# Queries and keys of a pair as one tile of 1024 columns in two neighbouring banks, and the cosine product placed behind the scaling of the scores on VectorE

## The chip, the cores and the metric

The kernel runs on one core of a Trainium2 chip. The metric is the device time of one execution in microseconds (us), and the time of a kernel is the median of its runs.

## What is computed

The reference is a macaron block on x of 8 sequences, 256 positions and 128 features, all in float32: half a transformer, a selective scan, and half a transformer with the same weights.

```python
x = x + 0.5 * _L0_ffn_ref(_layernorm(x, axis=-1), ...)
x = x + _L0_attn_ref(_layernorm(x, axis=-1), ...)
x = x + 0.5 * _L0_ffn_ref(_layernorm(x, axis=-1), ...)
```

`_L0_ffn_ref` is six layers, each an attention and a gated feed-forward layer. The attention is what the change touches:

```python
qkv = x @ Wqkv
q, k, v = jnp.split(qkv, 3, -1)
q = l2norm(q) * qs
k = l2norm(k) * ksc
q = q * cos * scale + rotate_half(q) * sin * scale
k = k * cos * inv + rotate_half(k) * sin * inv
out = local_attention(q, k, v)      # windows of 32, each sees itself and the one before
return out.transpose(0, 2, 1, 3).reshape(b, n, INNER) @ Wo
```

It has 16 heads of 64 features. `_L0_attn_ref` is layer norm, two projections, a short convolution, a scan over 16 states and an output projection.

## The kernel before

Features lie on the 128 partitions and tokens on the columns. The 2048 tokens are cut into 4 chunks of two sequences (512 columns). An **item** is one chunk in one layer, so that a stack (one of the two half transformers, k = 0 and 1) has 24 items. A **pair** is two heads, and an item has 8 pairs.

The whole stack is one pipeline of **steps**, 8 to an item, written out in advance: `Step(t)` says which piece of which item every engine does at step t, and each engine's program walks the same list (`tensor_stack`, `vector_stack`, `scalar_stack`, `gpsimd_stack`) in an order written by hand. The engines meet only through semaphores, and each takes its instructions strictly in this order. Step t projects pair p = t % 8 of item n = t // 8 (`st.now`). At every even step the attention of a **group** of four heads, projected 10 steps before, enters the pipeline:

- TensorE computes the scores (`pe_scores`, L719) onto banks that ScalarE has filled with the mask (`act_mask`, L1137).
- VectorE multiplies them by the inverse norms of the keys (`dve_scores`, L940) and takes the row maximum (`dve_max`, L946).
- Then follow GpSimd (subtract, scale), ScalarE (exponential, L1162), VectorE (`dve_sums`, L952), GpSimd again and the transpose `dve_turn` (L966), over the next steps.
- At the even step 4 steps later TensorE multiplies the probabilities by the values (`pe_values`, L692), and ScalarE copies the result (`act_att`, L1155).

What the text calls steps 0 to 7 is p. All even steps carry the scores of one group and the values of an earlier one. In addition, step 0 has the statistics of the norms of q and k on VectorE (`dve_norms`), step 1 `act_norms`, `dve_norms_back` (L922 to L927), half of the output projection (`pe_out`, L668) and the gates of the feed-forward layer; steps 2 and 3 the value half of it (`dve_hidden`, L973), step 4 its output (`pe_ffn_out`, added by L980 on VectorE), step 5 the other half of `pe_out`, steps 6 and 7 the layer norm.

For one pair and one step: TensorE projects the queries at the top of the step and the keys late in it (`pe_project`, three matmuls of 512 columns each, L656 to L658), each into one bank. ScalarE squares each (`act_square`, L1085). VectorE then makes two products out of each (`dve_rotate`): with the sine table into `sines` (L868), and with the cosine table into the ring of rotated queries or keys (L874). Four DMAs of SyncE move the sine products to their partner partitions, and GpSimd adds them (`pool_rotate`, L1259). Late in each step TensorE projects the values (`pe_v`, L749 to L751), and VectorE transposes them (`dve_v`, L891).

PSUM has 8 banks of 512 columns. One holds the sums of squares. The other seven are given out in a fixed rotation by the class `Banks`, in the order in which TensorE uses them: `use(key, sem, value)` gives the next bank and remembers which semaphore says that it has been read, and TensorE waits for the reader of the bank's last holder before it writes (`pe_bank`). `pe_values` takes four banks (one for each j) and waits for all four before its first matmul:

```python
            if blocks[0] == 0:
                for j in range(4):
                    pe_bank(w, ("att", k, n, group, j))
```

## Time and profile before

| | |
|---|---|
| median of 3 runs | 3368.71 us (3358.27 to 3374.22) |
| span of the profiled execution | 3373.6 us |
| TensorE busy | 2905.4 us (86%) |
| VectorE busy | 2981.4 us (88%) |
| GpSimd busy | 2425.2 us (72%) |
| ScalarE busy | 2061.4 us (61%) |

The profiled execution's own time is its span; it stands 4.9 us above the median of the runs. The busy shares are means over the whole span, with the scan between the two stacks in it (some 330 us), where other code runs. A matmul's record begins when it is taken up and its end is modelled, so that a busy TensorE is not TensorE at its peak.

### The profile page before, as it was taken

To read this page: it belongs to the slowest core of one execution; us is meant where nothing else is said; L and a number is where in the kernel's file an instruction comes from. 1 tells how busy PE (TensorE), PEld (TensorE's weight loads), DVE (VectorE), ACT (ScalarE), POOL (GpSimd) and SP (SyncE) were. 2 spreads that over 40 slices of the span, in tenths; PEclk is the share of its full clock that TensorE was granted. 3 is DMA by queue.
4 is the path that set the end of the run, shared out by engine and by line. 5 is a ranking of instruction groups with operands and counts; after the bars stand their busy time and mean duration, and the time that the engine had idled before them with its cause. 6 is when DMAs were issued, how large, how long until landed. Compare 5 with 4: busy or idle time off the path is not lost. (4 is left out here: it accounts for less than half of the span.)

```text
span 3373.6 us, 132100 instructions
## 1 busy us (share of the span) xinstructions
PE 2905.4 (86%) x57914; PEld 1846.3 (55%) x57914; DVE 2981.4 (88%) x4200; ACT 2061.4 (61%) x3820; POOL 2425.2 (72%) x1679
## 2 busy tenths in 40 slices
PE   5788889989989899987767788998999988999987
PEld 3455555655655555653323455565566655565653
DVE  6789899999999899896898878989999989899994
ACT  3466566666666665664764456666666666566663
POOL 3678777787787687774454667778788787787773
PEclk8899999999999999998887889999999999999998
DMA  5233332333333333320001333333343333333330
GB/s 140 65 83 73 82 91 68 89 90 72 86 92 71 84 85 71 83 72 28 7 7 44 80 72 79 75 87 86 75 97 76 90 84 72 81 94 71 86 76 14
DMA packets 114726, 250.85 MB, mean 74 GB/s; under 512 B 27244, under 2 KB 60648, under 8 KB 114152
## 3 DMA queue, kind: packets, MB, share of 16 engines
q1 hardware_dynamic: 114152, 242.40, 30.3%
q8 instruction: 457, 7.49, 1.0%
q14 instruction: 117, 0.96, 0.1%
HBM read 37.82 MB, written 3.15 MB: 12 GB/s over the span
## 5 line engine op out<-in xcount | busy, mean ns | idle before, releaser
L1085 ACT ACTIVATE squares<-general 128x512 f32<-128x512 f32 x768 | 453.9, 597 | 720.8 <-PE general L658 712.2
L1279 POOL TENSOR_TENSOR probs<-probs,row_sum 128x1024 f32<-128x1024 f32 x192 | 365.3, 1903 | 426.3 <-DVE row_sum L957 425.5
L1259 POOL TENSOR_TENSOR q_ring<-q_ring,partner 128x512 f32<-128x512 f32 x384 | 491.1, 1279 | 216.6 <-DMA partner<-sines 216.3
L868 DVE SCALAR_TENSOR_TENSOR sines<-general,vec,consts 128x512 f32<-128x512 f32 x768 | 560.7, 730 | 68.4 <-ACT squares L1085 65.5
L1259 POOL TENSOR_TENSOR k_ring<-k_ring,partner 128x512 f32<-128x512 f32 x384 | 490.8, 1278 | 0.0
L692 PE MATMUL general<-probs_t,v_buf 32*64 32x64 f32 x24576 | 339.4, 236 | 158.3 <-issue 87.0
L656 PE MATMUL general<-xs_hi,wqkv_lo 128*128 128x512 f32 x768 | 457.3, 595 | 15.8 <-DVE xs_lo L897 7.6
L692 PEld LDWEIGHTS general<-probs_t,v_buf 32*64 32x64 f32 x24576 | 305.6, 135 | 248.8 <-issue 241.7
L1273 POOL TENSOR_TENSOR probs<-probs,q_scale 128x1024 f32<-128x1024 f32 x192 | 365.3, 1903 | 15.1
L668 PE MATMUL general<-att,wo 128*128 128x512 f32 x768 | 370.4, 627 | 6.5 <-ACT att L1155 5.2
L719 PE MATMUL general<-k_ring,q_ring 64*32 64x64 f32 (+1 forms) x24576 | 294.2, 224 | 88.4 <-issue 53.5
L1265 POOL TENSOR_TENSOR probs<-probs,row_max 128x1024 f32<-128x1024 f32 x192 | 366.5, 1909 | 0.1
L719 PEld LDWEIGHTS general<-k_ring,q_ring 64*32 64x32 f32 x24576 | 260.0, 106 | 122.6 <-issue 103.4
L657 PE MATMUL general<-xs_lo,wqkv_hi 128*128 128x512 f32 x768 | 315.7, 411 | 2.7 <-issue 2.7
L658 PE MATMUL general<-xs_hi,wqkv_hi 128*128 128x512 f32 x768 | 314.5, 409 | 0.7 <-issue 0.5
L656 PEld LDWEIGHTS general<-xs_hi,wqkv_lo 128*128 128x128 f32 x768 | 153.7, 200 | 264.6 <-issue 233.4
L1155 ACT ACTIVATE att<-general 128x256 f32<-128x256 f32 x768 | 231.3, 388 | 97.0 <-PE general L692 95.6
L891 DVE STREAM_TRANSPOSE v_buf<-general 128x512 f32<-128x512 f32 x384 | 265.3, 691 | 27.1 <-PE general L751 27.0
L874 DVE SCALAR_TENSOR_TENSOR k_ring<-general,vec,consts 128x512 f32<-128x512 f32 x384 | 285.1, 742 | 0.0
L874 DVE SCALAR_TENSOR_TENSOR q_ring<-general,vec,consts 128x512 f32<-128x512 f32 x384 | 284.6, 741 | 0.0
L730 PE MATMUL sums<-squares,consts 128*32 128x512 f32 x1536 | 248.4, 612 | 40.4 <-ACT squares L1085 36.1
L952 DVE TENSOR_REDUCE row_sum<-probs 128x16 f32<-128x1024 f32 x192 | 230.6, 1201 | 41.2 <-ACT probs L1162 41.0
(232 smaller groups left out, 6348.2 us busy)
## 6 DMA issues: line engine op xcount, KB each, us to landing
partner<-sines SPq DMA_DIRECT2D x1536, 128.0 KB, 2.3
wqkv_raw<-in_wqkv SPq DMA_DIRECT2D x80, 208.0 KB, 2.7
wo<-in_wo SPq DMA_DIRECT2D x12, 512.0 KB, 5.1
w<-in_w SPq DMA_DIRECT2D x12, 341.0 KB, 3.2
base_dram<-x SPq DMA_DIRECT2D x8, 256.0 KB, 2.4
att<-in_wqkv SPq DMA_DIRECT2D x2, 1024.0 KB, 6.1
sines<-base_dram SPq DMA_DIRECT2D x8, 256.0 KB, 4.0
w<-in_w SPq DMA_DIRECT2D x12, 128.0 KB
```

What stands on the lines that cost most here:

```text
L656: e.matmul(g[:, :], wqkv_lo[:, p, cut], xs_hi[:, r, :], start=True, stop=False)
L657: e.matmul(g[:, :], wqkv_hi[:, p, cut], xs_lo[:, r, :], start=False, stop=False)
L668: done = e.matmul(g[:, :], wo[:, p, :], att[:, p, :], start=(p == OUT_PAIRS[i][0]), stop=(p == OUT_PAIRS[i][-1]))
L692: done = e.matmul(o, lhs, rhs, start=(kb == 0), stop=True, skip_group_check=True)
L719: done = e.matmul(o, qw, kw, start=False, stop=True, skip_group_check=True)
L868: e.scalar_tensor_tensor(out=by_seq(sines[:, i % 2, which, :]), in0=g, scalar=scale, in1=both(tables[:, 2 * which + 1, :]), op0=ALU.mult, ...
L874: e.scalar_tensor_tensor(out=by_seq(qk_ring[which][:, slot_of(n, p), :]), in0=g, scalar=scale, in1=both(tables[:, 2 * which, :]), op0=ALU. ...
L1085: e.activation(squares[:, (2 * p + which) % 4, :], general_of(("proj", k, n, p, which))[:, :], ACT.Square).then_inc(S[f"squared_{side}"], 1)
L1259: e.tensor_tensor(y, y, partner[:, i % 2, which, :], ALU.add).then_inc(S[f"rotated_{side}"], 1)
L1265: e.tensor_tensor(y, y, spread_keys(row_max[:, i % 2, :]), ALU.subtract).then_inc(S["max_off"], 1)
L1273: e.tensor_tensor(y, y, spread_keys(q_scale8[:, n % 2, group, :]), ALU.mult).then_inc(S["q_norms_off"], 1)
L1279: e.tensor_tensor(y, y, spread_keys(row_sum[:, i % 2, :]), ALU.mult).then_inc(S["probs_done"], 1)
```

## The change

The queries and keys of a pair become one tile of 1024 columns. `Banks.use` takes a width: a tile of two banks needs two neighbours (and skips the last bank of the rotation where only that one is left), and its first matmul waits for the readers of both. TensorE projects queries and keys directly behind each other at the top of the step, with one signal behind both. ScalarE squares both in one instruction, and GpSimd adds the partners of both in one. On VectorE the scale vector moves into a copy of the tables, made once a layer (`dve_tables`, two instructions), so that each product is a plain multiplication, and one instruction makes the sine products of both (`dve_sin`), another the cosine products (`dve_cos`). `dve_cos` stands behind `dve_scores`, which in turn is one instruction of 1024 columns instead of two of 512; the mask copy likewise. The two banks of the projection are released by the semaphore `cos`. To make room, `inv_norm` and two weights of the scan share memory with other tiles, and the loads of the scan's weights stand at the end of SyncE's list of the first stack.

```diff
-    def use(self, key, sem, value):
-        at = self.next
-        self.next = (at + 1) % self.banks
-        self.of[key], self.before[key], self.filled[key] = at, self.last.get(at), self.written.get(at, False)
-        self.last[at] = (sem, value)
-        self.written[at] = key[0] in ("proj", "v", "spread", "scores", "project", "ffn_out", "center", "var")\
-            or key[0] in ("gate", "value") and HIDDEN_CUTS[key[3]][1] == P
+    def use(self, key, sem, value, width=1):
+
+        at = self.next if self.next + width <= self.banks else 0
+        self.next = (at + width) % self.banks
+        taken = range(at, at + width)
+        self.of[key], self.before[key] = at, [self.last[i] for i in taken if i in self.last]
+        self.filled[key] = all(self.written.get(i, False) for i in taken)
+        for i in taken:
+            self.last[i] = (sem, value)
+            self.written[i] = key[0] in ("proj", "v", "spread", "scores", "project", "ffn_out", "center", "var")\
+                or key[0] in ("gate", "value") and HIDDEN_CUTS[key[3]][1] == P
...
-                self.use(("proj", k, n, p, 0), "cos_q", (g + n) * PAIRS + p + 1)
+                self.use(("proj", k, n, p), "cos", (g + n) * PAIRS + p + 1, 2)
...
-                for seq in range(CHUNK_SEQS):
-                    self.use(("scores", k, n, group, seq), "k_norms_off", ((g + n) * GROUPS + group) * 2 + seq + 1)
+                self.use(("scores", k, n, group), "k_norms_off", (g + n) * GROUPS + group + 1, CHUNK_SEQS)
...
-            if st.now:
-                n, p = st.now
-                self.use(("proj", k, n, p, 1), "cos_k", (g + n) * PAIRS + p + 1)
...
-        qk_ring = [sb("q_ring", [P, RING, COLS]), sb("k_ring", [P, RING, COLS])]
+        qk_ring = sb("qk_ring", [P, RING, 2, COLS])
+        layer_tables = sb("layer_tables", [P, 2, 2, SEQ])
...
+        inv_norm = k_inv[:, WIN:]
...
+        ring = banks("general", POOL_BANKS)
+        general = [ring[:, i * COLS:(i + 1) * COLS] for i in range(POOL_BANKS)]
+        sums = banks("sums", 1)
...
-        mw = sb("mw", [P, 4, P])
-        wbc = sb("wbc", [P, P])
+        raw_words = wqkv_raw.rearrange("p i c -> p (i c)")
+        mw = raw_words[:, 0:4 * P].rearrange("p (m n) -> p m n", m=4)
+        wbc = raw_words[:, 4 * P:5 * P]
...
+        def two_of(key):
+            at = BANKS.index(key)
+            return ring[:, at * COLS:(at + 2) * COLS]
...
+            if k == 0:
+                w.wait_ge(S["wqkv_lo"], DEPTH * PAIRS)
+                e.dma_start(mw, mw_in.rearrange("m d n -> d m n")).then_inc(S["m_loaded"], 16)
+                e.dma_start(wbc, wb_in).then_inc(S["m_loaded"], 16)
+                e.dma_start(mvec[:, :], mvec_in).then_inc(S["m_loaded"], 16)
...
-            w.wait_ge(S["sin_q"], i + 1)
-            w.wait_ge(S["sin_k"], i + 1)
-
-            w.wait_ge(S["rotated_q"], i - 1)
-            w.wait_ge(S["rotated_k"], i - 1)
+            w.wait_ge(S["sin"], i + 1)
+
+            w.wait_ge(S["rotated"], i - 1)
...
         def pe_bank(w, key):
-            before = BANKS.free(key)
-            if before:
-                w.wait_ge(S[before[0]], before[1])
+            for sem, value in BANKS.free(key):
+                w.wait_ge(S[sem], value)
             return general_of(key)
...
-        def pe_project(e, w, k, n, p, which):
+        def pe_project(e, w, k, n, p):
+
             m, r = k * ITEMS + n, n % 2
-            g, cut = pe_bank(w, ("proj", k, n, p, which)), slice(which * P, (which + 1) * P)
+            pe_bank(w, ("proj", k, n, p))
             w.wait_ge(S["xs_lo"], m + 1)
             w.wait_ge(S["wqkv_lo"], (k * DEPTH + n // CHUNKS) * PAIRS + p + 1)
-            e.matmul(g[:, :], wqkv_lo[:, p, cut], xs_hi[:, r, :], start=True, stop=False)
-            e.matmul(g[:, :], wqkv_hi[:, p, cut], xs_lo[:, r, :], start=False, stop=False)
-            e.matmul(g[:, :], wqkv_hi[:, p, cut], xs_hi[:, r, :], start=False, stop=True)\
-                .then_inc(S[f"proj_{SIDE[which]}"], 1)
+            for which in range(2):
+                g, cut = two_of(("proj", k, n, p))[:, which * COLS:(which + 1) * COLS], slice(which * P, (which + 1) * P)
+                e.matmul(g, wqkv_lo[:, p, cut], xs_hi[:, r, :], start=True, stop=False)
+                e.matmul(g, wqkv_hi[:, p, cut], xs_lo[:, r, :], start=False, stop=False)
+                done = e.matmul(g, wqkv_hi[:, p, cut], xs_hi[:, r, :], start=False, stop=True)
+            done.then_inc(S["proj"], 1)
...
                 if st.now:
-                    pe_project(e, w, k, *st.now, 0)
+                    pe_project(e, w, k, *st.now)
...
-                if st.now:
-                    pe_project(e, w, k, *st.now, 1)
                 if st.values:
...
-        def dve_rotate(e, w, k, n, p, which):
-            m, side, layer = k * ITEMS + n, SIDE[which], n // CHUNKS
-            i = m * PAIRS + p
-            g, scale = by_seq(general_of(("proj", k, n, p, which))[:, :]), vcol(layer, V_QS + which)
+        def by_side(a):
+            return a.rearrange("p w (s t) -> p w s t", s=CHUNK_SEQS)
+
+        def layer_table(part):
+            return layer_tables[:, :, part, :].unsqueeze(2).broadcast_to([P, 2, CHUNK_SEQS, SEQ])
+
+        def dve_tables(e, w, k, layer):
+
             w.wait_ge(S["vec_loaded"], 16)
-            w.wait_ge(S[f"squared_{side}"], i + 1)
+            w.wait_ge(S["cos"], (k * ITEMS + layer * CHUNKS) * PAIRS)
+            for which in range(2):
+                e.tensor_scalar(layer_tables[:, which, :, :], tables[:, which, :, :], vcol(layer, V_QS + which), None, ALU.mult)\
+                    .then_inc(S["tables_scaled"], 1)
+
+        def dve_sin(e, w, k, n, p):
+            i = (k * ITEMS + n) * PAIRS + p
+            if p == 0 and n % CHUNKS == 0:
+                dve_tables(e, w, k, n // CHUNKS)
+            w.wait_ge(S["tables_scaled"], 2 * (k * DEPTH + n // CHUNKS + 1))
+            w.wait_ge(S["squared"], i + 1)
 
             w.wait_ge(S[f"moved{i % 2}"], i // 2 * 64)
-            e.scalar_tensor_tensor(out=by_seq(sines[:, i % 2, which, :]), in0=g, scalar=scale, in1=both(tables[:, 2 * which + 1, :]),
-                                   op0=ALU.mult, op1=ALU.mult).then_inc(S[f"sin_{side}"], 1)
+            g = by_side(two_of(("proj", k, n, p)).rearrange("p (w c) -> p w c", w=2))
+            e.tensor_tensor(by_side(sines[:, i % 2, :, :]), g, layer_table(1), ALU.mult).then_inc(S["sin"], 1)
+
+        def dve_cos(e, w, k, n, p):
+            g = by_side(two_of(("proj", k, n, p)).rearrange("p (w c) -> p w c", w=2))
 
             held = n * PAIRS + p - RING
             if held >= 0:
                 w.wait_ge(S["scored"], (k * ITEMS + held // PAIRS) * GROUPS + held % PAIRS // 2 + 1)
-            e.scalar_tensor_tensor(out=by_seq(qk_ring[which][:, slot_of(n, p), :]), in0=g, scalar=scale,
-                                   in1=both(tables[:, 2 * which, :]), op0=ALU.mult, op1=ALU.mult).then_inc(S[f"cos_{side}"], 1)
+            e.tensor_tensor(by_side(qk_ring[:, slot_of(n, p), :, :]), g, layer_table(0), ALU.mult).then_inc(S["cos"], 1)
...
-            for seq in range(CHUNK_SEQS):
-                start = k_inv[:, seq * SEQ:seq * SEQ + 1]
-                keys = bass.AP(start.tensor, start.offset, [list(start.ap[0]), [WIN, NWIN], [1, 2 * WIN]])
-                y = probs[:, i % PROBS, seq * COLS:(seq + 1) * COLS]
-                e.tensor_tensor(cube(y), cube(general_of(("scores", k, n, group, seq))[:, :]), keys, ALU.mult).then_inc(S["k_norms_off"], 1)
+            start = k_inv[:, 0:1]
+            keys = bass.AP(start.tensor, start.offset, [list(start.ap[0]), [WIN, ITEM_WINS], [1, 2 * WIN]])
+            e.tensor_tensor(cube(probs[:, i % PROBS, :]), cube(two_of(("scores", k, n, group))), keys, ALU.mult).then_inc(S["k_norms_off"], 1)
...
                 if st.now:
-                    dve_rotate(e, w, k, *st.now, 0)
+                    dve_sin(e, w, k, *st.now)
                 if st.scale:
                     dve_scores(e, w, k, *st.scale)
+                if st.now:
+                    dve_cos(e, w, k, *st.now)
...
-                if st.now:
-                    dve_rotate(e, w, k, *st.now, 1)
...
-        def act_square(e, w, k, n, p, which):
-            i, side = (k * ITEMS + n) * PAIRS + p, SIDE[which]
-            w.wait_ge(S[f"proj_{side}"], i + 1)
+        def act_square(e, w, k, n, p):
+            i, at = (k * ITEMS + n) * PAIRS + p, 2 * (p % 2)
+            w.wait_ge(S["proj"], i + 1)
             w.wait_ge(S["squares_summed"], i // 2)
-            e.activation(squares[:, (2 * p + which) % 4, :], general_of(("proj", k, n, p, which))[:, :], ACT.Square).then_inc(S[f"squared_{side}"], 1)
+            e.activation(squares[:, at:at + 2, :].rearrange("p w c -> p (w c)"), two_of(("proj", k, n, p)), ACT.Square).then_inc(S["squared"], 1)
...
-        def pool_rotate(e, w, k, n, p, which):
-            i, side = (k * ITEMS + n) * PAIRS + p, SIDE[which]
-            y = qk_ring[which][:, slot_of(n, p), :]
+        def pool_rotate(e, w, k, n, p):
+            i = (k * ITEMS + n) * PAIRS + p
+            y = qk_ring[:, slot_of(n, p), :, :]
             w.wait_ge(S[f"moved{i % 2}"], (i // 2 + 1) * 64)
-            w.wait_ge(S[f"cos_{side}"], i + 1)
-            e.tensor_tensor(y, y, partner[:, i % 2, which, :], ALU.add).then_inc(S[f"rotated_{side}"], 1)
```

TensorE at step 2 of an item in the middle of a stack. L764 is the first matmul of the feed-forward layer's value half, L656 to L658 are the projection of the keys, L692 is `pe_values`, L749 the projection of v. Before:

```order
L764 MATMUL general<-centered,w 128x512 [waits gelu_done]
L656 MATMUL general<-xs_hi,wqkv_lo 128x512 [waits cos_k]
L657 MATMUL general<-xs_lo,wqkv_hi 128x512
L658 MATMUL general<-xs_hi,wqkv_hi 128x512
L692 MATMUL general<-probs_t,v_buf 64x64 [waits k_inv_kept,cos_q,k_norms_off,v_kept,probs_turned]
L692 MATMUL general<-probs_t,v_buf 64x64 x55
L692 MATMUL general<-probs_t,v_buf 64x32 x8
L749 MATMUL general<-xs_hi,wqkv_lo 128x256 [waits k_norms_off]
```

After the change (L741 is the spread of the norms, L722 the scores, L767 the value half, L696 `pe_values`, L752 the projection of v):

```order
L741 MATMUL general<-inv_parts,spread_sel 128x256
L722 MATMUL general<-qk_ring 32x32 [waits mask_set,rotated]
L722 MATMUL general<-qk_ring 32x32 x7
L722 MATMUL general<-qk_ring 32x64 x56
L767 MATMUL general<-centered,w 128x512 [waits gelu_done]
L696 MATMUL general<-probs_t,v_buf 64x64 [waits cos,k_inv_kept,v_kept,probs_turned]
L696 MATMUL general<-probs_t,v_buf 64x64 x55
L696 MATMUL general<-probs_t,v_buf 64x32 x8
L752 MATMUL general<-xs_hi,wqkv_lo 128x256 [waits k_norms_off]
```

The projection of the keys is gone from the place between the value half and `pe_values`; it stands at the top of the step. Among the semaphores for which `pe_values` waits, `cos` of this same step stands where `cos_q` and `k_norms_off` of this step stood.

VectorE at step 4, from the top of the step. L868 and L874 are the sine and cosine products, L940 is `dve_scores`, L980 adds the feed-forward output, L952 is `dve_sums`, L891 `dve_v`. Before:

```order
L868 SCALAR_TENSOR_TENSOR sines<-general,vec,consts 128x512 [waits moved0,squared_q]
L874 SCALAR_TENSOR_TENSOR q_ring<-general,vec,consts 128x512
L940 TENSOR_TENSOR probs<-general,k_inv 128x512 [waits k_inv_kept,probs_turned,scored]
L940 TENSOR_TENSOR probs<-general,k_inv 128x512
L980 SCALAR_TENSOR_TENSOR x<-general,vec,x 128x512 [waits shifted,ffn_done]
L868 SCALAR_TENSOR_TENSOR sines<-general,vec,consts 128x512 [waits squared_k]
L874 SCALAR_TENSOR_TENSOR k_ring<-general,vec,consts 128x512
L952 TENSOR_REDUCE row_sum<-probs 128x16 [waits exponent]
L891 STREAM_TRANSPOSE v_buf<-general 128x16x32 [waits v_projected]
L957 RECIPROCAL row_sum<-row_sum 128x16 [waits row_sum]
```

After the change (L884 and L892 are the sine and cosine products, L955 `dve_scores`, L995 the addition, L967 `dve_sums`, L908 `dve_v`):

```order
L884 TENSOR_TENSOR sines<-general,layer_tables 128x1024 [waits moved0,squared]
L955 TENSOR_TENSOR probs<-general,k_inv 128x1024 [waits k_inv_kept,probs_turned,scored]
L892 TENSOR_TENSOR qk_ring<-general,layer_tables 128x1024
L995 SCALAR_TENSOR_TENSOR x<-general,vec,x 128x512 [waits shifted,ffn_done]
L967 TENSOR_REDUCE row_sum<-probs 128x16 [waits exponent]
L908 STREAM_TRANSPOSE v_buf<-general 128x16x32 [waits v_projected]
L972 RECIPROCAL row_sum<-row_sum 128x16 [waits row_sum]
L961 TENSOR_REDUCE row_max<-probs 128x16 [waits max_off,k_norms_off]
```

Four products of 512 columns became two of 1024; the cosine product moved from ahead of the scaling of the scores to behind it.

## Rows read from the trace of the kernel before

**Rows 1.** Windows of core 0: busy us of each engine, granted clock, DMA share, GB/s

```profile
20.00:170.00 150.00, 103.23 (x1642) 68.27 (x1642) 115.72 (x174) 67.91 (x137) 81.81 (x59) 0.84 0.36 85
300.00:1400.00 1100.00, 990.41 (x21260) 645.92 (x21259) 1010.48 (x1440) 706.97 (x1333) 849.11 (x583) 0.96 0.35 81
```

**Rows 2.** Groups of VectorE by form, 300 to 1400 us: count | busy, mean ns | idle before

```profile
L868 DVE SCALAR_TENSOR_TENSOR sines<-general,vec,consts 128x512 f32<-128x512 f32 x284 | 207.4, 730 | 14.1 <-ACT squares L1085 13.0
```

**Rows 3.** Timeline of VectorE, 899 to 960 us: start, duration, instruction, [idle before it <-releaser]

```profile
899.77 1.28 DVE L940 TENSOR_TENSOR probs<-general,k_inv 128x512 f32<-128x512 f32 x2
...
903.87 1.22 DVE L952 TENSOR_REDUCE row_sum<-probs 128x16 f32<-128x1024 f32 x1 [0.84 <-ACT probs L1162]
...
913.82 1.28 DVE L940 TENSOR_TENSOR probs<-general,k_inv 128x512 f32<-128x512 f32 x2
915.01 0.74 DVE L980 SCALAR_TENSOR_TENSOR x<-general,vec,x 128x512 f32<-128x512 f32 x1
915.67 0.74 DVE L868 SCALAR_TENSOR_TENSOR sines<-general,vec,consts 128x512 f32<-128x512 f32 x1
916.33 0.75 DVE L874 SCALAR_TENSOR_TENSOR k_ring<-general,vec,consts 128x512 f32<-128x512 f32 x1
916.99 1.21 DVE L952 TENSOR_REDUCE row_sum<-probs 128x16 f32<-128x1024 f32 x1
918.11 0.71 DVE L891 STREAM_TRANSPOSE v_buf<-general 128x512 f32<-128x512 f32 x1
...
918.87 1.17 DVE L946 TENSOR_REDUCE row_max<-probs 128x16 f32<-128x1024 f32 x1
919.95 0.74 DVE L868 SCALAR_TENSOR_TENSOR sines<-general,vec,consts 128x512 f32<-128x512 f32 x1
...
927.12 1.28 DVE L940 TENSOR_TENSOR probs<-general,k_inv 128x512 f32<-128x512 f32 x2
...
932.63 0.72 DVE L891 STREAM_TRANSPOSE v_buf<-general 128x512 f32<-128x512 f32 x1 [0.90 <-PE general L751]
...
941.23 1.28 DVE L940 TENSOR_TENSOR probs<-general,k_inv 128x512 f32<-128x512 f32 x2
...
950.59 1.00 DVE L922 CAST norm_t<-norm_t 128x128 fp32r<-128x128 f32 x1
...
959.10 1.28 DVE L940 TENSOR_TENSOR probs<-general,k_inv 128x512 f32<-128x512 f32 x2
```

**Rows 4.** Timeline of TensorE, 935 to 949 us: start, duration, instruction

```profile
935.50 1.08 PE L730 MATMUL sums<-squares,consts 128*32 128x512 f32 x8
936.51 0.50 PE L656 MATMUL general<-xs_hi,wqkv_lo 128*128 128x512 f32 x1
...
937.64 1.48 PE L719 MATMUL general<-k_ring,q_ring 64*32 64x32 f32 x128
...
941.57 1.57 PE L692 MATMUL general<-probs_t,v_buf 32*64 32x64 f32 x128 [1.56 <-DVE q_ring L874]
943.07 0.39 PE L749 MATMUL general<-xs_hi,wqkv_lo 128*128 128x256 f32 x1
...
943.88 0.40 PE L656 MATMUL general<-xs_hi,wqkv_lo 128*128 128x512 f32 x1
...
944.58 3.65 PE L668 MATMUL general<-att,wo 128*128 128x512 f32 x8
```

**Rows 5.** Timeline of ScalarE, 941 to 950 us: start, duration, instruction

```profile
941.95 1.06 ACT L1162 ACTIVATE probs<-probs 128x1024 f32<-128x1024 f32 x1
...
944.78 0.60 ACT L1085 ACTIVATE squares<-general 128x512 f32<-128x512 f32 x1 [0.36 <-PE general L658]
945.39 1.28 ACT L1112 ACT_TABLE_LOAD   x1
...
948.66 0.31 ACT L1115 ACTIVATE norm_t<-norm_t 128x128 f32<-128x128 f32 x1
```

93 lines of the change are left out of this document (40 added, 53 removed).

## The prediction

> **What bounds the kernel now.** I read the windows first. From 300 to 1400 us, in the middle of the first stack, VectorE is busy 1010.48 of 1100 us and TensorE 990.41, with the clock granted at 0.96 on average (its levels are 1.2 and 2.4 GHz); ScalarE with 706.97 and GpSimd with 849.11 have room [rows 1]. The sine products number 284 in this stretch, two a step: 142 steps, 7.75 us each, 62.0 us an item [rows 2].
>
> Which of the two sets the end is seen in VectorE's timeline. Take the starts of the scaling (L940) as the beat: 899.77 at step 2, 913.82 at step 4, 927.12 at step 6, 941.23 at step 0, 959.10 at step 2 of the next item [rows 3]. The distances are 14.05, 13.30, 14.11 and 17.87 us. Almost all of it is one instruction behind the other; the waits of note are 0.84 us in the first distance and 0.90 us in the third. Without them it is 13.21 + 13.30 + 13.21 + 17.87 = 57.6 us an item. So VectorE bounds an undisturbed item at 57.6, and the other 4.4 of the 62.0 are waits for others. TensorE runs ahead: at step 0 it stands for 1.56 us before `pe_values`, until VectorE's cosine product of the queries, made at the top of the same step, gives a bank free [rows 4]. That is the place to watch.
>
> **What the change takes from VectorE.** A product of 512 columns costs 0.66 us from start to start (915.67 to 916.33 to 916.99), and there are four a step: 2.64 us. The two scalings take 1.19 us (913.82 to 915.01), 0.60 each. A row maximum over 1024 columns takes 1.08 (918.87 to 919.95) [rows 3]. No row has a product of 1024 columns. Its bounds are 1.08, as the maximum, and 1.32, two of today's products with nothing gained; the nearest row is the scaling, also a plain multiplication out of PSUM, which gives 1.19 for two halves, less the cost of one start. I take 1.13. A step then saves 2.64 − 2.26 = 0.38 us, a scaling 0.06, so two steps save 0.82 us, an item 3.3 us. The tables of a layer are two instructions for 4 items; nothing.
>
> The Trainium skill, VectorE: DVE Perf Modes, section on the TRN2 errata, says that a fixed cost is paid per instruction, so that one large tile pays it once; by its row 120 + FD cycles at 0.96 GHz for PSUM sources a merged pair would save 0.13 us, and an item 20 × 0.13 = 2.5 us. The rows give somewhat more in sum, since the plain product is also cheaper than the one with a scale.
>
> **What it adds: a wait on both sides.** After the change `pe_values` takes, of its four banks, two or one that held this step's projection, and so waits for `cos` of this very step. By the rotation that holds for 180 of the 192 groups. And `cos` stands behind the scaling, which waits for this step's scores. Call the end of the cosine product of an even step zero, and follow both engines.
>
> TensorE: `pe_values` starts 0.34 later (941.23, the end of the cosine product's slot, to 941.57), lasts 1.50 (to 943.07), the projection of v 0.81 (to 943.88), both projections 2 × 0.70 (943.88 to 944.58 is one) [rows 4], the way to ScalarE 0.20 (944.58 to 944.78), the square of 1024 columns 1.06, as the exponential of that width (one of 512 is 0.60) [rows 5]. Sum: 0.34 + 1.50 + 0.81 + 1.40 + 0.20 + 1.06 = 5.31 us until VectorE may begin the sine product of the next step. Today the same way is 0.70 + 0.46 shorter, and it starts earlier, at the cosine product of the queries or the first half of the scaling, with 1.31 us of key products still ahead of VectorE.
>
> VectorE itself has between these two points, at steps 2, 4 and 6, an extra piece (0.66 for L980), the row sums 1.12, v and the reciprocal 0.76, the maximum 1.08: 3.62 us [rows 3]. It waits 5.31 − 3.62 = 1.69 us, where it waited for nothing. Queued behind it are the next pair's products, the transpose of the probabilities, and all that TensorE needs for the next beat.
>
> The four beats after the change:
> - Step 2 to 4: 13.21 − 0.82 + 1.69 = 14.1 us, +0.9.
> - Step 6 to 0: the same, +0.9.
> - Step 4 to 6: TensorE has half of the output projection in it, and its own way is longer than VectorE's. From zero: 0.34 + 1.50 + 0.81 + 1.40, the output projection 3.5 (a record of 3.65 that overlaps its neighbour), v 0.81, sums 1.01, both projections 1.40 [rows 4], then 0.20 + 1.06 to the sine product of step 6, and there sine, scaling and cosine 3 × 1.13 = 3.39: 15.4 us against 13.30, +2.1. The scores (1.48 long, L719) fit beside the square and the sine product.
> - Step 0 to 2: VectorE has the statistics of the norms there, more than the 5.31. But `dve_norms_back` waits for ScalarE, which stands behind the square: the square ends at 5.31, table load to root take 945.39 to 948.97 = 3.58 [rows 5], so 8.89. VectorE is there at 950.59 − 941.23 = 9.36, less scaling 1.19 and four products 2.64, plus two of 1.13: 7.8; it waits 1.1. From there today's next scaling begins 959.10 − 950.59 = 8.51 later, with the key products of step 1 and the query products of step 2 (2.62) in between; with these out and one sine product, scaling and cosine product (3.39) in, it is 9.3. Sum 18.2 against 17.87, +0.3.
>
> Together +4.2 us an item. The first two items of each stack are not yet full, so 44 of 48 count: 44 × 4.2 = 185 us. The profiled execution's own time is 3373.6, 4.9 above the median of the runs: 3373.6 + 185 − 4.9 = 3554, and I say 3555 us. I leave the 4.4 us of other waits as they are.
>
> **Edits at nothing.** Squares in one instruction and additions on GpSimd in one: both engines have room as above, and what the wider square delays is in the 5.31. GpSimd's additions feed scores only 8 steps and more later. The four DMAs of a pair start once, after the sine product of both, earlier in the step than the keys' was; if that cover failed, scores would be late by the DMA, with some 60 us in between. SyncE's three loads moved past all the stack's partner moves are waited for once, between stack and scan; no row prices that wait, and I bound it by nothing and one step, 7.75 us. The aliased `inv_norm` waits only for scalings that VectorE has already made in its own order. The mask copy of a group waits for both banks, at most the second's reader.
>
> **Rivals.**
> *Faster: VectorE stays the bound.* If TensorE's answer fits into VectorE's own work, the 3.3 us an item are won: 44 × 3.3 = 145, 3224 us. For it speaks how full VectorE is; against it the sum 5.31 against 3.62. It decides at the point where the way over TensorE and ScalarE falls below 3.6 us; for that every link would have to be a third shorter. Chance 0.15.
>
> *Same: new and old waits coincide.* Each item has 4.4 us of waits already. The new ones, 4.2 + 3.3 = 7.5 us, may cover them, as an engine that stands still anyway is not delayed by a late neighbour. If all 4.4 are covered, +4.2 − 4.4 = −0.2 us an item, 3360 us. Against it: the old ones come from TensorE being late, and it now has less slack to make up for it. Chance 0.12.
>
> *Slower still: the clock.* From 20 to 170 us, where TensorE is busy 103.23 of 150, the granted clock is 0.84 [rows 1]. TensorE stands longer before `pe_values` after the change. On the way that now counts lie some 18 us of its work an item (3 × 3.7 and 6.7 in step 4 to 6); at 0.84 instead of 0.96 they take 18 × 0.14 = 2.6 us more: 44 × 2.6 = 113, 3668 us. The Trainium skill, TensorE: Matmul & The Clock Gate, section "A second HAM failure mode: psum-queue depth-cycling", tells of a kernel that cycled through PSUM banks and whose short pauses between groups of matmuls made the clock swing between its levels; by that rule this case is the likely one. The trace bears it out in so far as the less busy stretch has the lower clock. Chance 0.13.
>
> **Chances and range.** 0.60 for my forecast. Its own range: an item has 20 wide instructions; at 1.08 each they take 1.0 us less in all, −44; at 1.32 they take 3.8 us more, of which about half lies where VectorE does not wait anyway, +84. So 3510 to 3640, and down to 3450 if half of the old waits are covered. For 8 in 10 I leave out the faster rival and the top of the clock's: 3350 to 3690. What a measurement of this kernel can tell from no change is about 0.5%, 17 us. Faster by more: 0.16 (the first rival and a little of the second). Within: 0.07, out of the second. Slower: 0.77.
>
> **What would show it.** Right: VectorE's sine product waits for ScalarE's square at steps 3, 5 and 7, some 1.7 us each; TensorE waits for the cosine product before `pe_values` at nearly every even step; VectorE's share of busy time falls below 85% in the middle of a stack; the beats are near 14, 15, 14 and 18 us when nothing disturbs. Wrong: VectorE still without gaps and beats of 12.4, 12.5, 12.4 and 17.0, or a wide product that isn't near 1.13 from start to start. The forecast rests most on `pe_values` being unable to start before `cos`: if other work hides that wait, it falls.

## The result and the profile after

The changed kernel takes 3802.01 us (median of 4, 3787.92 to 3803.95), the kernel before 3370.97 in the same runs: ratio 1.129, interval [1.125, 1.133], some 431 us slower. I had said 3555, and at most 3690: the sign was right, the size less than half.

The same window of the changed kernel, to be read against [rows 1]:

```profile
core 0: us, PE busy (x) PEld busy (x) DVE busy (x) ACT busy (x) POOL busy (x), PEclk, DMA share, GB/s
300.00:1400.00 1100.00, 896.39 (x18442) 602.92 (x18442) 880.42 (x945) 588.61 (x967) 714.96 (x382) 0.89 0.30 71
```

VectorE and TensorE both fall, from 1010.48 and 990.41 to 880.42 and 896.39 of 1100 us: no engine is full any more, both stand in turn. The granted clock falls from 0.96 to 0.89.

VectorE's groups in the same stretch (busy us, mean ns of one | idle before them), against [rows 2]:

```profile
L884 DVE TENSOR_TENSOR sines<-general,layer_tables 128x1024 f32<-128x1024 f32 x124 | 150.7, 1215 | 94.1 <-ACT squares L1100 94.0
L892 DVE TENSOR_TENSOR qk_ring<-general,layer_tables 128x1024 f32<-128x1024 f32 x123 | 149.1, 1212 | 0.0
L908 DVE STREAM_TRANSPOSE v_buf<-general 128x512 f32<-128x512 f32 x124 | 85.8, 692 | 73.1 <-PE general L754 72.9
...
L955 DVE TENSOR_TENSOR probs<-general,k_inv 128x1024 f32<-128x1024 f32 x62 | 75.2, 1213 | 17.2 <-PE general L722 16.2 <-ACT k_inv L1159 1.1
...
L914 DVE TENSOR_TENSOR xs_lo<-xs,xs_hi 128x512 fp32r<-128x512 f32 x15 | 37.5, 2500 | 0.0
...
L941 DVE TENSOR_TENSOR norm_t<-norm_t 128x128 f32<-128x128 f32 x15 | 27.4, 1828 | 0.5
...
L939 DVE CAST norm_t<-norm_t 128x128 fp32r<-128x128 f32 x15 | 15.8, 1050 | 18.7 <-ACT norm_t L1130 18.7
L847 DVE TENSOR_SCALAR norm_t<-norm_t 128x16 f32<-128x16 f32 x15 | 15.3, 1021 | 0.5
```

The 62 scalings (L955) make 15.5 items, so an item takes 71.0 us where it took 62.0. Its work is the same: 1010.48 / 17.75 = 56.9 us busy before, 880.42 / 15.5 = 56.8 after. The idle time is what grew, from 5.0 to 14.2 us an item. What released VectorE in that stretch, and TensorE before `pe_values`, in the kernel before and then in the changed one (us in total, times, longest):

```profile
DVE x L904 <- PE general L668: 17.5, 18, 2.4
DVE sines L868 <- ACT squares L1085: 13.0, 27, 1.2
DVE v_buf L891 <- PE general L751: 11.8, 13, 2.5
...
PE general L692 <- DVE q_ring L874: 20.5, 14, 2.5
```

```profile
DVE sines L884 <- ACT squares L1100: 94.0, 90, 2.9
DVE v_buf L908 <- PE general L754: 72.9, 43, 4.1
DVE norm_t L939 <- ACT norm_t L1130: 18.7, 15, 1.3
DVE probs L955 <- PE general L722: 16.2, 9, 3.0
...
PE general L696 <- DVE qk_ring L892: 136.7, 56, 6.9
```

Waits for the squares went from 13.0 / 17.75 = 0.7 to 94.0 / 15.5 = 6.1 us an item, waits for the projection of v from 0.7 to 4.7, and TensorE's wait for the cosine product from 20.5 / 17.75 = 1.2 to 136.7 / 15.5 = 8.8. All waits for v and 53.4 of the 94.0 us (59 of the 90 times, added up from the timeline) lie between an even step's cosine product and the next odd step's sine product, where the prediction put the new wait for steps 2, 4 and 6 (16.4 of the 53.4 lie behind step 0, where it put none); the other 40.5 lie ahead of an even step's sine product: 30.4 at step 6, as 1039.17 below, where it put one, and 10.1 at step 2, where it put none.

VectorE's timeline (start, duration, instruction, [idle before <- releaser]), against [rows 3]; L955 is the scaling, so its starts are the beats:

```profile
1009.42 1.22 DVE L955 TENSOR_TENSOR probs<-general,k_inv 128x1024 f32<-128x1024 f32 x1
1010.55 1.22 DVE L892 TENSOR_TENSOR qk_ring<-general,layer_tables 128x1024 f32<-128x1024 f32 x1
1011.68 0.74 DVE L988 SCALAR_TENSOR_TENSOR hidden<-general,vec,hidden 128x512 f32<-128x512 f32 x1
...
1015.39 0.72 DVE L908 STREAM_TRANSPOSE v_buf<-general 128x512 f32<-128x512 f32 x1 [1.85 <-PE general L754]
...
1018.45 1.22 DVE L884 TENSOR_TENSOR sines<-general,layer_tables 128x1024 f32<-128x1024 f32 x1 [1.12 <-ACT squares L1100]
...
1023.79 1.18 DVE L884 TENSOR_TENSOR sines<-general,layer_tables 128x1024 f32<-128x1024 f32 x1
1024.90 1.20 DVE L955 TENSOR_TENSOR probs<-general,k_inv 128x1024 f32<-128x1024 f32 x1
1026.03 1.20 DVE L892 TENSOR_TENSOR qk_ring<-general,layer_tables 128x1024 f32<-128x1024 f32 x1
1027.16 0.73 DVE L995 SCALAR_TENSOR_TENSOR x<-general,vec,x 128x512 f32<-128x512 f32 x1
...
1030.00 0.72 DVE L908 STREAM_TRANSPOSE v_buf<-general 128x512 f32<-128x512 f32 x1 [0.99 <-PE general L754]
...
1032.54 1.23 DVE L884 TENSOR_TENSOR sines<-general,layer_tables 128x1024 f32<-128x1024 f32 x1 [0.60 <-ACT squares L1100]
...
1039.17 1.22 DVE L884 TENSOR_TENSOR sines<-general,layer_tables 128x1024 f32<-128x1024 f32 x1 [1.91 <-ACT squares L1100]
1040.31 1.21 DVE L955 TENSOR_TENSOR probs<-general,k_inv 128x1024 f32<-128x1024 f32 x1
...
1042.57 2.75 DVE L914 TENSOR_TENSOR xs_lo<-xs,xs_hi 128x512 fp32r<-128x512 f32 x1
...
1058.45 1.22 DVE L955 TENSOR_TENSOR probs<-general,k_inv 128x1024 f32<-128x1024 f32 x1 [0.23 <-ACT k_inv L1159]
```

Three things stand here. A wide product takes 1.13 to 1.14 us from start to start (1023.79, 1024.90, 1026.03, 1027.16), as priced. The beats are 15.48 (step 2 to 4), 15.41 (4 to 6) and 18.14 us (6 to 0). And the way from the end of the cosine product to the next sine product is 1018.45 − 1011.68 = 6.77 us in the first beat, 1032.54 − 1027.16 = 5.38 in the second; the forecast says 5.31. TensorE in the same two beats, against [rows 4] (a row with x1 is one matmul):

```profile
1012.02 1.76 PE L696 MATMUL general<-probs_t,v_buf 32*64 32x64 f32 x128 [2.10 <-DVE qk_ring L892]
...
1014.52 0.41 PE L752 MATMUL general<-xs_hi,wqkv_lo 128*128 128x256 f32 x1
1014.73 0.41 PE L753 MATMUL general<-xs_lo,wqkv_hi 128*128 128x256 f32 x1
...
1015.16 0.63 PE L660 MATMUL general<-xs_hi,wqkv_lo 128*128 128x512 f32 x1
...
1016.01 0.63 PE L662 MATMUL general<-xs_hi,wqkv_hi 128*128 128x512 f32 x1
...
1027.49 1.56 PE L696 MATMUL general<-probs_t,v_buf 32*64 32x64 f32 x128 [0.57 <-DVE qk_ring L892]
...
1029.44 0.28 PE L752 MATMUL general<-xs_hi,wqkv_lo 128*128 128x256 f32 x1
1029.56 0.28 PE L753 MATMUL general<-xs_lo,wqkv_hi 128*128 128x256 f32 x1
...
1029.80 0.39 PE L660 MATMUL general<-xs_hi,wqkv_lo 128*128 128x512 f32 x1
1030.03 0.39 PE L661 MATMUL general<-xs_lo,wqkv_hi 128*128 128x512 f32 x1
```

Both times `pe_values` (L696) waits for `dve_cos` of its own step (L892) and starts about 0.34 us after its slot ends (1011.68 to 1012.02, 1027.16 to 1027.49). In the first case it stood 2.10 us, and afterwards the matmuls of 256 columns lie 0.21 us apart and those of 512 columns 0.43: the clock is at its lower level, 1.2 GHz (granted clock 1.00 from 1011 to 1013 us, 0.50 from 1014 to 1016, 1.00 again from 1017). In the second it stood 0.57, and they lie 0.12 and 0.23 apart: 2.4 GHz. That is the 1.4 us between 6.77 and 5.38. ScalarE adds its square of 1.02 us (against [rows 5]):

```profile
1017.39 1.02 ACT L1100 ACTIVATE squares<-general 128x1024 f32<-128x1024 f32 x1 [2.36 <-PE general L662]
```

Over the 40 such ways behind each of steps 2, 4 and 6 (all items but the first four of each stack), the shortest is 5.29, 5.28 and 5.29 us, but the median 6.7, 5.5 and 6.8 and the mean 7.0, 6.5 and 7.2. Behind steps 2 and 6 nearly all of the difference between mean and shortest lies in TensorE's three pieces, `pe_values`, the projection of v and the two projections: 1.65 of 1.66 us and 1.80 of 1.88.

The subtraction `xs_lo` at 1042.57 takes 2.75 us; [rows 3] and the group of before have no such length at that place: 902 ns in the mean. GpSimd's timeline around it:

```profile
1042.43 2.35 POOL L1273 TENSOR_TENSOR qk_ring<-qk_ring,partner 128x1024 f32<-128x1024 f32 x1
```

GpSimd's joined addition ends at 1044.78, and the subtraction only 0.5 us later. In the mean the addition takes 2386 ns in the stretch, where each of the two before took 1278:

```profile
L1273 POOL TENSOR_TENSOR qk_ring<-qk_ring,partner 128x1024 f32<-128x1024 f32 x123 | 292.6, 2386 | 0.2
```

The experiments take this up.

### The profile page after: what moved, and what is told of

It reads as the page before. It is cut to its first block, busy times and chain, and to the rows that moved or that the text cites. A ratio compares the mean times of both kernels' runs of the same rounds, so it can differ in the third digit from the quotient of the medians.

```text
span 3800.3 us, 129724 instructions
## 1 busy us (share of the span) xinstructions
PE 3004.3 (79%) x57916; PEld 1967.1 (52%) x57916; DVE 2983.8 (79%) x3264; ACT 1995.5 (53%) x3252; POOL 2359.6 (62%) x1295
## 4 chain that ended last, share of the span: by engine, by line
PE 42%; DVE 28%; issue 15%; ACT 12%; POOL 2%; DMA 1%; SPq 0%; DVEq 0%; POOLq 0%; ACTq 0%
PE general L696 9%; DVE qk_ring L892 7%; ACT squares L1100 5%; PE general L672 5%; DVE probs L955 5%; PE general L660 4%; PE general L661 4%; PE general L662 3%; PE general L752 3%; DVE sines L884 3%; PE general L774 2%; PE general L753 2%; PE general L754 2%; PE sums L733 2%; DVE probs_t L981 2%
## 5 line engine op out<-in xcount | busy, mean ns | idle before, releaser
L1273 POOL TENSOR_TENSOR qk_ring<-qk_ring,partner 128x1024 f32<-128x1024 f32 x384 | 913.4, 2385 | 75.8 <-DMA partner<-sines 75.4
L696 PE MATMUL general<-probs_t,v_buf 32*64 32x64 f32 x24576 | 370.1, 268 | 463.5 <-DVE qk_ring L892 406.6
L884 DVE TENSOR_TENSOR sines<-general,layer_tables 128x1024 f32<-128x1024 f32 x384 | 466.8, 1216 | 323.6 <-ACT squares L1100 319.2
L696 PEld LDWEIGHTS general<-probs_t,v_buf 32*64 32x64 f32 x24576 | 345.3, 162 | 594.9 <-issue 588.1
L1100 ACT ACTIVATE squares<-general 128x1024 f32<-128x1024 f32 x384 | 391.4, 1019 | 406.1 <-PE general L662 405.0
L892 DVE TENSOR_TENSOR qk_ring<-general,layer_tables 128x1024 f32<-128x1024 f32 x384 | 465.5, 1212 | 0.0
L908 DVE STREAM_TRANSPOSE v_buf<-general 128x512 f32<-128x512 f32 x384 | 265.6, 692 | 215.4 <-PE general L754 214.8
L1287 POOL TENSOR_TENSOR probs<-probs,q_scale 128x1024 f32<-128x1024 f32 x192 | 365.7, 1905 | 15.0
L722 PE MATMUL general<-qk_ring 64*32 64x64 f32 (+1 forms) x24576 | 287.0, 225 | 106.7 <-issue 70.9
L752 PE MATMUL general<-xs_hi,wqkv_lo 128*128 128x256 f32 x768 | 350.3, 456 | 10.3 <-issue 10.3
L722 PEld LDWEIGHTS general<-qk_ring 64*32 64x32 f32 x24576 | 253.1, 106 | 146.0 <-issue 132.4
L1152 ACT ACTIVATE general<-mask_bf 128x1024 f32<-128x1024 bf16 x182 | 186.6, 1025 | 247.0 <-DVE hidden L988 127.5
L955 DVE TENSOR_TENSOR probs<-general,k_inv 128x1024 f32<-128x1024 f32 x192 | 232.9, 1213 | 51.3 <-PE general L722 49.3
L753 PE MATMUL general<-xs_lo,wqkv_hi 128*128 128x256 f32 x768 | 248.3, 323 | 2.4 <-issue 2.4
```

What stands on the lines that cost most here:

```text
L696: done = e.matmul(o, lhs, rhs, start=(kb == 0), stop=True, skip_group_check=True)
L722: done = e.matmul(o, qw, kw, start=False, stop=True, skip_group_check=True)
L752: e.matmul(g[:, cut], wqkv_lo[:, p, cols], xs_hi[:, r, cut], start=seq == 0, stop=False, skip_group_check=True)
L884: e.tensor_tensor(by_side(sines[:, i % 2, :, :]), g, layer_table(1), ALU.mult).then_inc(S["sin"], 1)
L892: e.tensor_tensor(by_side(qk_ring[:, slot_of(n, p), :, :]), g, layer_table(0), ALU.mult).then_inc(S["cos"], 1)
L955: e.tensor_tensor(cube(probs[:, i % PROBS, :]), cube(two_of(("scores", k, n, group))), keys, ALU.mult).then_inc(S["k_norms_off"], 1)
```

## The experiments

Each ratio is to the kernel before, run on the same chip in turns. The first four undo the change bit by bit, starting from the changed kernel.

**Cosine product ahead of the scaling.**

```diff
                     dve_sin(e, w, k, *st.now)
+                    dve_cos(e, w, k, *st.now)
                 if st.scale:
                     dve_scores(e, w, k, *st.scale)
-                if st.now:
-                    dve_cos(e, w, k, *st.now)
```

> The changed kernel with one thing undone: VectorE makes the cosine product directly behind the sine product, ahead of the scaling of the scores. Theory A (the wait of the attention output for this step's cosine product, behind scores and scaling, is most of the loss): TensorE's wait before the attention output nearly goes, the granted clock comes back to 0.94 or more, and the time falls to 3350 to 3500 us. Rival C (what costs is that additions of 1024 columns on GpSimd hold up VectorE instructions whose operands all lie in SBUF): the time stays within 60 us of 3802. Rival D (both projections at the top of the step and the long way over the square of 1024 columns to the sine product are the loss, whatever the order of the cosine): the time stays above 3700, and VectorE's waits for the squares stay near 320 us.

3600.23 us, ratio 1.0685 [1.065, 1.072]: 200 us or 6.1 points come back, the largest single part. TensorE's wait for `cos` before `pe_values` falls from 136.7 to 92.8 us in 300 to 1400, VectorE's for v from 72.9 to 28.8; that for the squares falls little (94.0 to 80.2). No theory's range holds: A had the right largest part, but put the time at 3350 to 3500 and the wait of `pe_values` near nothing, and the clock comes back to 0.91, not 0.94.

**GpSimd's addition in two halves**, alone and with the edit above.

```diff
-            e.tensor_tensor(y, y, partner[:, i % 2, :, :], ALU.add).then_inc(S["rotated"], 1)
+            for which in range(2):
+                y = qk_ring[:, slot_of(n, p), which, :]
+                done = e.tensor_tensor(y, y, partner[:, i % 2, which, :], ALU.add)
+            done.then_inc(S["rotated"], 1)
```

> The changed kernel with GpSimd's addition of the partners as two instructions of 512 columns, one behind the other, in the same place. Theory C (VectorE's instructions with all operands in SBUF stand until GpSimd's instruction ends, which now lasts 2.4 us instead of 1.3): the split of the tokens on VectorE (2.45 us on average in the middle of a stack, 0.90 before the change) falls to 1.5 or less, the addition of epsilon from 1.0 to 0.5 or less, and the time falls by 1.5 to 3 us an item, 70 to 140 us. Theory A (all is the wait for the cosine product): less than 20 us.

> Both edits in the changed kernel: cosine product ahead of the scaling, GpSimd's addition in two halves. Theory A with C beside it: faster than either alone, 3250 to 3420 us; if VectorE is the bound again, the beats of two steps are 12.5, 12.5, 12.5 and 17 us when nothing disturbs, and the time is below that of the kernel before the change. Rival D: above 3600.

3745.44 us, ratio 1.112 [1.108, 1.117], and with the cosine product first 3537.89, ratio 1.051 [1.046, 1.055]. The halves are worth 57 and 62 us: a part by itself, that I had put at nothing, if somewhat less than the 70 of Theory C. `xs_lo` falls from 2500 ns to 1622 and 1630, but the addition of eps only from 1021 to 893 alone, and with the cosine product first it is at 1201. Both edits together miss their range by over 100 us (3250 to 3420 expected): something more is lost.

**And the square and the sine product by side**, on top of both; only the cosine product and the scaling are still 1024 wide.

```diff
-            w.wait_ge(S["proj"], i + 1)
-            e.activation(squares[:, at:at + 2, :].rearrange("p w c -> p (w c)"), two_of(("proj", k, n, p)), ACT.Square).then_inc(S["squared"], 1)
+            for which, (proj, squared) in enumerate((("proj_q", "squared_q"), ("proj", "squared"))):
+                w.wait_ge(S[proj], i + 1)
+                e.activation(squares[:, at + which, :], two_of(("proj", k, n, p))[:, which * COLS:(which + 1) * COLS], ACT.Square)\
+                    .then_inc(S[squared], 1)
...
+            for which, (squared, sin) in enumerate((("squared_q", "sin_q"), ("squared", "sin"))):
+                w.wait_ge(S[squared], i + 1)
```

> The changed kernel with the cosine product right behind the sine product and GpSimd's addition in halves (3538 us), and in addition TensorE signals each of the two projections, ScalarE squares each by itself and VectorE makes two sine products of 512 columns; the cosine product stays 1024 wide. Theory W (what is left over the kernel with the keys at the top, 3437 us, is the way over both projections and one long square, which the joined instruction makes VectorE wait for): the sine products end some 0.9 us earlier after the projections, which counts at the 3 steps of an item where VectorE waits: 2.7 us an item, 130 us in all, 3410 to 3450 us; VectorE's wait for squares falls from 5.1 us an item to under 3. Theory B (it is the release of both banks at once and the pairs of banks): 3520 to 3550 us, and VectorE only waits one instruction later.

3424.61 us, ratio 1.017 [1.013, 1.021]: 113 us come back, in the range of Theory W. VectorE's wait for the squares falls from 85.4 us (16.75 items, 5.1 each) to 38.1 (17.5 items, 2.2 each):

```profile
DVE v_buf L909 <- PE general L754: 38.9, 39, 3.9
DVE sines L885 <- ACT squares L1101: 38.1, 50, 2.5
```

Joining the two sides makes VectorE wait for both projections and one long square, where it could have begun on the queries' half. Not all of the 113 us need be that: `xs_lo` falls in the same run from 1630 to 960 ns and the addition of eps from 1201 to 666, though GpSimd's additions are as they were, so that they meet VectorE's instructions elsewhere. With the subtraction of the norms longer (1706 ns for 1448) that is some 1.0 us an item where 2.4 were won, and the run can't tell the two apart. What is left, 1.7 points, holds the keys' place and what is still joined; no run splits it. The keys' place was measured from the other side, and with it two more parts, each put into the kernel before:

**Keys at the top of the step in the kernel before**, 512 wide: projection, square and products of the keys stand directly behind those of the queries.

```diff
                 if st.now:
                     dve_rotate(e, w, k, *st.now, 0)
+                    dve_rotate(e, w, k, *st.now, 1)
```

> The kernel before the change with tiles and instructions of 512 columns as they were, but the keys' projection, square and products directly behind the queries' at the top of the step, ahead of the scaling of the scores; GpSimd's additions as they were. Theory P (position: with all rotation work at the top, nothing of it is left to cover TensorE's way from the attention output to the next square, and banks of this step's projection are what the attention output waits for): 4 to 7% slower than before, near the kernel with the cosine first and the addition in halves (3538). Theory W (width: the wide square and the wide products, of which nothing can start until both halves are done, are what is lost there): within 1.5% of before.

3436.58 us, ratio 1.023 [1.019, 1.027]: between the two theories (4 to 7%, and within 1.5%). Here too the cast of the norms (1329 ns, 898 before) and the addition of eps (742, 212 before) are longer than before, so that the 2.3 points are not the place alone.

**Queries' cosine product behind the scaling in the kernel before**, everything else as it was.

```diff
-                    dve_rotate(e, w, k, *st.now, 0)
+                    dve_rotate(e, w, k, *st.now, 0, (0,))
                 if st.scale:
                     dve_scores(e, w, k, *st.scale)
+                if st.now:
+                    dve_rotate(e, w, k, *st.now, 0, (1,))
```

> The kernel before the change with one thing moved: VectorE's cosine product of the queries (512 columns) behind the scaling of the scores instead of ahead of it. Theory A' (the place behind the scaling is harmful by itself): the attention output waits 1.3 us longer at each even step, and the time rises by over 1.5%. Theory A'' (it costs only when the keys' work is not left in the late place to cover it): VectorE keeps its cover of 1.3 us of key products, and the time stays within 1% of before.

3503.16 us, ratio 1.045 [1.040, 1.050]. One instruction of 0.66 us, moved past two of 0.60, costs 146 us. That is 3.0 us an item, where the move delays the bank by 1.2 us at 4 steps, 4.8 an item. TensorE's wait before `pe_values` for that product rises from 20.5 us ([rows 4] has one of 1.56) to 47.3 in 300 to 1400. A part is GpSimd's again: `xs_lo` takes 1396 ns here (902 before) and the cast 1234 (898), 0.8 us an item together.

**Joined addition in the kernel before.** GpSimd adds queries and keys in one instruction, for which both rings become one tile, and which has to wait for the keys' cosine product too; the other engines' instructions stay as they are.

```diff
+            w.wait_ge(S["cos_q"], i + 1)
+            w.wait_ge(S["cos_k"], i + 1)
+            e.tensor_tensor(y, y, partner[:, i % 2, :, :], ALU.add).then_inc(S["rotated_q"], 1)
```

> The kernel before the change with queries and keys in one ring and GpSimd's two additions of 512 columns joined into one of 1024, in the queries' place; everything else as before. Theory C (VectorE's instructions with all operands in SBUF stand until GpSimd's instruction is over): the split of the tokens (0.90 us on average, half of them near 0.69) and the norm instructions get longer, by 1 to 3 us an item in sum, and since VectorE bounds this kernel the time rises by 40 to 140 us. Rival: no change of over 0.5%, if in this order the two instructions seldom meet.

3422.35 us, ratio 1.019 [1.016, 1.023]. VectorE's groups of that kernel (300 to 1400):

```profile
L920 DVE CAST norm_t<-norm_t 128x128 fp32r<-128x128 f32 x17 | 23.9, 1407 | 10.1 <-ACT norm_t L1113 10.1
...
L844 DVE TENSOR_SCALAR norm_t<-norm_t 128x16 f32<-128x16 f32 x18 | 16.9, 936 | 0.6
...
L895 DVE TENSOR_TENSOR xs_lo<-xs,xs_hi 128x512 fp32r<-128x512 f32 x18 | 12.3, 684 | 0.0
```

The cast of the norms takes 1407 ns (898 before), the addition of eps 936 (212 before); `xs_lo` takes 684 (902 before). Theory C holds in the time (65 us, 40 to 140 expected), but it had `xs_lo` longer.

**The addition over 8 columns** of 512 a side, in the changed kernel: the rotation is left out of the others.

```diff
-            e.tensor_tensor(y, y, partner[:, i % 2, :, :], ALU.add).then_inc(S["rotated"], 1)
+            e.tensor_tensor(y[:, :, 0:8], y[:, :, 0:8], partner[:, i % 2, :, 0:8], ALU.add).then_inc(S["rotated"], 1)
```

> The changed kernel with GpSimd's addition over 8 of the 512 columns of each side, so that the rotation is left out of the other columns; it measures the cost of the addition itself. Theory G (an instruction of VectorE whose operands all lie in SBUF stands until GpSimd's running instruction ends): the subtraction xs_lo falls from 2500 ns to about 700, the subtraction of the norms (L941) from 1828 to under 500, the addition of eps from 1021 to about 230, the cast from 1050 to about 350: some 5 us an item less on VectorE, of which the waits for TensorE give back a part; 3600 to 3680 us. Theory H (these instructions are long by themselves, or their length is covered by other waits): their times stay, or the time stays within 1% of 3802.

3715.85 us, ratio 1.104 [1.100, 1.108]. The mechanism is there, instruction by instruction:

```profile
L847 DVE TENSOR_SCALAR norm_t<-norm_t 128x16 f32<-128x16 f32 x16 | 17.4, 1089 | 0.6
...
L914 DVE TENSOR_TENSOR xs_lo<-xs,xs_hi 128x512 fp32r<-128x512 f32 x16 | 14.0, 877 | 0.0
...
L939 DVE CAST norm_t<-norm_t 128x128 fp32r<-128x128 f32 x16 | 6.6, 415 | 19.8 <-ACT norm_t L1130 19.8
L941 DVE TENSOR_TENSOR norm_t<-norm_t 128x128 f32<-128x128 f32 x16 | 4.7, 292 | 0.6
```

`xs_lo` from 2500 to 877 ns, the subtraction of the norms (L941) from 1828 to 292, the cast from 1050 to 415. The addition of eps (L847) stays at 1089: in the whole run 41 of its 56 begin while GpSimd scales the probabilities (L1287), an instruction as long as before. But the time falls by 86 us, not by the 120 and more that Theory G expected: VectorE's waits for squares and v rise from 166.9 to 203.6 us, so that much of that length lay where VectorE would have waited anyway. All of the addition, with its length, costs 86 us; joining it costs 57.

**Whole pair in the late place**, addition in halves: projection, square and products of both sides, 1024 wide, where the keys' were.

```diff
                 if st.scale:
                     dve_scores(e, w, k, *st.scale)
...
+                if st.now:
+                    dve_sin(e, w, k, *st.now)
+                    dve_cos(e, w, k, *st.now)
```

> The changed kernel with the pair's projection, square, sine and cosine products, still 1024 columns wide, all in the late place where the keys' were before the change (on TensorE ahead of the attention output, on VectorE behind the extra pieces of the step and ahead of the transpose of the probabilities), and GpSimd's addition in two halves. By the rotation the attention output then waits for this step's scaling, not for its cosine product. Theory P (position): VectorE has the scaling and the extra pieces as cover for the projection and the square, the wide instructions keep their gain, and the time is 3230 to 3420 us, at or below before. Theory W (width): slower than 3480 us all the same.

3574.94 us, ratio 1.065 [1.061, 1.069]. Theory W holds (over 3480). `pe_values` no longer waits for the cosine product; TensorE waits for it in other places, 17.1 us ahead of the projection, 16.0 ahead of the value half and 11.1 ahead of the layer norm's matmul, 44.2 in all where the early place with the same width had 94.7. The granted clock is 0.98 in 300 to 1400 (0.946 over the span, 0.938 before), and yet it is slower than that early place (3537.89). VectorE waits 87.9 us for the squares, mostly at steps 1, 2, 4 and 6, and 37.7 for the output projection. So neither the late place nor the clock repairs the width.

**Filler matmuls** in the changed kernel: eight of 512 bf16 columns ahead of `pe_values`' wait for its other banks, for three groups of four (in the trace they lie around steps 4, 6 and 0, not at 0, 2 and 6 as I had expected); the bank is overwritten behind them.

```diff
+                pe_bank(w, ("att", k, n, group, 0))
+                if group != 2:
+                    for _ in range(8):
+                        e.matmul(g[0][:, :], ident_bf[:, :], mask_bf[:, :], start=True, stop=True, skip_group_check=True)
```

> The changed kernel with 8 matmuls more of 512 columns in bfloat16 (mask times identity, about 1.7 us at the full clock) in steps 0, 2 and 6 on TensorE, written into the first bank of the attention output ahead of its wait for the other banks; the attention output overwrites them. They fill part of the pause before the attention output. Theory B (the pauses bring the clock down, and the low clock is over half of what the forecast missed): the granted clock rises from 0.88 to 0.93 or more in the middle of a stack, and the time falls by 80 us or more in spite of the added work. Theory A alone, with the clock a bystander: the time stays within 40 us of 3802, or rises.

3757.62 us, ratio 1.115 [1.110, 1.121]. The granted clock rises from 0.88 to 0.93 over the span and 44 us come back, which lies just outside A's 40 and well short of B's 80. At step 6, where the filler mostly runs while TensorE stood anyway, the mean of the way from cosine to sine product falls from 7.2 to 5.8 us; at step 4 it rises from 6.5 to 7.2, since the filler (1.89 us) starts only behind the cosine product. VectorE's instructions that meet GpSimd's got no shorter (`xs_lo` 2445 ns, the addition of eps 1616), so the gain isn't theirs. I therefore take the 44 us for less than the clock's share, as the filler itself costs time; the run doesn't say how much less.

**Is VectorE's time worth its length before?** Two kernels take work from VectorE in the kernel before and leave its order of steps and the banks alone. The first multiplies the tables by the scale once a layer and has plain products, 512 wide (it is also the one that could have beaten the kernel before; it shares memory and moves the scan's loads as the change does):

```diff
-            e.scalar_tensor_tensor(out=by_seq(sines[:, i % 2, which, :]), in0=g, scalar=scale, in1=both(tables[:, 2 * which + 1, :]),
-                                   op0=ALU.mult, op1=ALU.mult).then_inc(S[f"sin_{side}"], 1)
+            e.tensor_tensor(by_seq(sines[:, i % 2, which, :]), g, both(layer_tables[:, 2 * which + 1, :]), ALU.mult).then_inc(S[f"sin_{side}"], 1)
```

> The kernel before with the layer's tables multiplied by the scale once a layer, and its four products of 512 columns a step as plain multiplications (TENSOR_TENSOR in place of SCALAR_TENSOR_TENSOR); nothing is joined, and neither the order nor the banks change. The two plain scalings of 512 columns in the kernel before lie 0.60 us apart, the products with a scale 0.66. Theory V (VectorE sets the time of an undisturbed item, so what is taken from it there is won): 32 products an item by 0.06 us are 1.9 us, some 1.6 after the tables are paid; 48 items give 75 us: 3290 us, ratio 0.978. Theory S (TensorE's answer is so near that VectorE then waits instead): 3355 to 3375, ratio 0.995 to 1.0.

3392.89 us, ratio 1.008 [1.006, 1.011]: a small loss, outside both theories. The product falls to 671 ns (from 730), and scaling the tables takes 1174 ns each, 1.0 us an item:

```profile
L877 DVE TENSOR_TENSOR sines<-general,layer_tables 128x512 f32<-128x512 f32 x285 | 191.3, 671 | 19.9 <-ACT squares L1092 19.1
...
L871 DVE TENSOR_SCALAR layer_tables<-consts,vec 128x256 f32<-128x256 f32 x16 | 17.8, 1174 | 0.0
```

The four scalings stand together, ahead of the layer's first products, so that the bank comes free late: at step 0 `pe_values` waits 5.7 us in the mean in the first item of a layer, and 1.7 in the other items. Over the ten layers whose pipeline is full that is 40 us. This run is therefore no clean test of Theory V. The changed kernel has the same with its two scalings, 5.8 us against 4.0, some 18 us in all: the tables were not "nothing".

The second halves both reductions, over a window's own 32 keys, so that half of each row sum is left out; then the same in the changed kernel.

```diff
-            e.tensor_reduce(row_max[:, i % 2, :], cube(probs[:, i % PROBS, :]), AX.X, ALU.max)
+            e.tensor_reduce(row_max[:, i % 2, :], cube(probs[:, i % PROBS, :])[:, :, WIN:2 * WIN], AX.X, ALU.max)
```

> The kernel before with both reductions of a group (row maximum, row sum) over the 32 columns of a window's own keys in place of all 64, so that half of the row sum is left out. Each reduction of 1024 columns takes 1.08 us from start to start; half the columns are worth some 0.53 us, two a group and four groups an item: 4.3 us an item less on VectorE, nothing else is changed. Theory V (a clean item is VectorE's 57.6 us; my forecast rests on this where it lets 3.3 us an item come off the time): 48 x 4.3 = 206 us, 3155 to 3200 us. Theory S (TensorE's own chain is nearly as long, so that VectorE's time falls and its waits grow; then the forecast should have had no saving in it): more than half of it turns into waits, 3265 us or more.

> The same in the changed kernel: both reductions over 32 of 64 columns of a window, half of the row sum left out. Theory R (after the change VectorE waits for TensorE and ScalarE behind every cosine product, and the two reductions lie inside that wait or beside it): less than a quarter of the 206 us is won, 3750 us or more. Theory V: VectorE's work still sets most of the item, 3600 to 3680 us.

Before: 3288.06 us, ratio 0.976 [0.973, 0.979], 79 us of the 206 are won, near the 3265 and more of Theory S. Changed kernel: 3786.25, ratio 1.124 [1.121, 1.127], 16 of 206, as Theory R had it. The rest turns into waits. In the kernel before, the wait for the squares goes from 13.0 to 32.8 us, that for the output projection from 17.5 to 24.1:

```profile
DVE sines L868 <- ACT squares L1085: 32.8, 63, 2.0
DVE x L904 <- PE general L668: 24.1, 19, 2.0
```

Theory V is refuted by both of these: a microsecond less on VectorE was worth about 0.4 before the change, and less than 0.1 after it.

## Why the prediction was right in sign and wrong in size

Right, by its own steps:
- The wide product's 1.13 us: 1.13 to 1.14 measured.
- The new wait of `pe_values` on this step's `cos`, at nearly every even step: 136.7 us of it in 300 to 1400, 56 times for 62 groups. The place of the cosine product behind the scaling alone makes 200 of the 431 us.
- The sum 5.31 us for the way over TensorE and ScalarE: 5.28 to 5.29 where nothing disturbs. The beats 14.1 and 15.4 us are the shortest seen, 14.00 for step 2 to 4 and 15.40 for 4 to 6.
- The item of 57.6 us before: the shortest of each of the four beats add up to 57.4.
- VectorE's share in the middle of a stack below 85%: 880.42 / 1100 = 80%.

Wrong. The forecast's item was 61.8 us undisturbed (14.1 + 15.4 + 14.1 + 18.2) and 4.4 of other waits, 66.2. In the 44 full items it takes 71.8 in the mean (62.0 before, both added up from the timelines' beats), and 44 × 9.7 = 427 us is the whole loss. The shortest of its four beats are 14.00, 15.40, 15.79 and 19.27, 64.5 in sum, and what comes on top is 7.3 us (4.6 before). So of the 5.6 us that the forecast lacks, 2.7 are in the undisturbed beats 6 to 0 and 0 to 2, where the short instructions stand that GpSimd delays (with the addition over 8 columns these two are 14.83 and 18.46), and 2.9 in the waits. By its terms:
- **"I leave the 4.4 us of other waits as they are."** This is the step that failed, together with the next one: the forecast took the way over TensorE and ScalarE at its shortest, 5.31 us, in every item, and the other waits as they were. Medians of the beats, without the first four items of each stack, are 16.3, 15.6, 16.6 and 20.5 us where I said 14.1, 15.4, 14.1 and 18.2. A good part is the clock: at 1.2 GHz the same way takes 1.4 us longer. I had that as a rival, priced 2.6 us an item, chance 0.13, and treated it as an alternative to the forecast; it comes on top of it, whenever the new wait is long.
- **The 3.3 us an item on VectorE, taken from the waits as won.** The undisturbed item was VectorE's, but TensorE's chain was close behind: halved reductions won 79 of 206 us. By that rate the 3.3 us were worth 1.3, by the changed kernel's (16 of 206) 0.3. And nearly all of what came off the products and the scaling was given back elsewhere on VectorE, whose busy time stayed at 56.9 and 56.8: 2.7 us in `xs_lo` and the four short instructions on `norm_t`, 0.4 in the tables.
- **GpSimd's joined addition, under "Edits at nothing".** I asked whether GpSimd has room, not what its longer instruction does to VectorE. It costs 57 to 62 us in the changed kernel, and 1.9% in the kernel before. In the changed kernel `xs_lo` (2500 ns against 902) and the eps addition (1021 against 212) alone are 2.4 us an item longer in the mean.
- **The joined square and sine product, counted only as length** ("today the same way is 0.70 + 0.46 shorter"). I had that in the 5.31 of steps 2, 4 and 6, and took it for small; undone, it gives 113 us, 2.4 us an item, of which a part may be GpSimd's delay as said above.
- **"The tables of a layer are two instructions for 4 items; nothing."** Some 18 us, as worked out above.

The undoing in sequence gives the sum of the parts: ratio 1.129, less 6.1 points for the cosine product behind the scaling, 1.8 for the joined addition, 3.4 for the joined square and sine product, 1.7 left, for the keys' place and what is still joined. The shares depend on the order in which they are taken: put into the kernel before one at a time, the first, second and fourth cost 4.5, 1.9 and 2.3 points.

Of the rivals, "faster" and "new and old waits coincide" are out. "The clock" was right as a mechanism: 0.94 to 0.88 over the span. The Trainium skill, TensorE: Matmul & The Clock Gate, section "A second HAM failure mode: psum-queue depth-cycling", names this pattern, short pauses between groups of matmuls while banks are handed round, and the trace agrees: 0.43 against 0.23 us for 512 columns, after pauses of 2.10 and 0.57. But a loss of this kind doesn't need the clock: the late place had 0.98 in 300 to 1400 and was 6.5% slower.

What stays open: how much of the 431 us is the clock's own. The filler run gives 44 us, and less than the whole. An estimate from the changed kernel's trace: of the 88 ways behind steps 2 and 6 of full items, 16 had the full clock from `pe_values` on and took 5.9 and 5.6 us in the mean, the other 72 took 7.3 and 7.4. That is 2.6 us an item, 115 us in all, if nothing else sets these ways apart and all of it counts. Nor is it shown why one moved instruction (3.0 us an item) costs more in the changed kernel (4.2 us an item, 202 / 48) than in the kernel before, where moreover the instruction is half as wide.

## What to carry to other kernels

Joining two instructions saves a start and adds two dependences: the first half waits for the second half's input (the square and the sine product here), and the first half's buffer is freed with the second's (no run prices this one by itself). Price both before the saving. A longer instruction on GpSimd can lengthen VectorE's even where GpSimd has room. Where two engines are within a few per cent of each other, take off only part of what is saved on the fuller one (0.4 here), but count all of what is added to the way between them. And an instruction behind one that waits for another engine inherits that wait: ask who is waiting for it before moving it there.

## What the runs showed of the hardware

- Some of VectorE's instructions with all operands in SBUF stand while GpSimd's runs: `xs_lo` takes 877 ns beside the addition over 8 columns, 1622 beside two of 512 and 2500 beside one of 1024, the subtraction of the norms 292, 1188 and 1828; In the whole changed run 44 of the 48 `xs_lo` begin while an instruction of GpSimd's runs and take 2381 ns in the mean, the 4 that meet none 681. The same holds for the addition of eps (979 against 182) and the cast (1472 against 221). Not all stand: row maximum and row sum (1159 to 1201 ns), the reciprocals (208 to 211 and 952 to 954) and the transpose of the probabilities (1220 to 1235) keep their time in all these runs, though their operands lie in SBUF too. So do products and scalings of 1024 columns, whose input is in PSUM (1211 to 1217). The Trainium skill, SBUF — State Buffer, section "SBUF: two separate sides", says so: the port pair that VectorE shares with GpSimd is an exclusive lock, held for a whole instruction, and taken by VectorE's instructions with two SBUF inputs or in a 2-port mode. The trace agrees for the subtractions, which have two SBUF inputs, and it shows the stand as length of the instruction, not as a wait. The prediction would have had its warning there.
- A wide addition on GpSimd saves 7% over two: 2386 ns against 2 × 1278.
- After a pause of 2.10 us TensorE fell to 1.2 GHz (granted clock 0.50 from 1014 to 1016 us, the pause having ended at 1012.02) and was back at 2.4 by 1017; after one of 0.57 it stayed at 2.4. Such a pause doesn't always do it: at steps 2 and 6 of the 44 full items it is 2.0 and 2.2 us in the mean, and in 16 of the 88 cases the clock stayed at 2.4 on the whole way to the next sine product.
